# Flamingo block with WKV and a mixture of experts on one core: keys and y turned on VectorE by way of a scratch in memory

## The reference, cut to what matters

```python
def reference(x, ctx, g_xattn, g_ffn, time_decay, time_first, router, w_up_gate, w_down, shared_w_up_gate, shared_w_down):
    # x, ctx: (16, 256, 512)
    k = _layernorm(x)
    # WKV: per batch element and channel a scan over the 256 steps
    #   y_t = (a + exp(u + k_t) v_t) / (b + exp(u + k_t)),  a, b decayed sums of exp(k) v and exp(k)
    x = x + tanh(g_xattn) * _wkv(time_decay, time_first, k, ctx)
    z = _layernorm(x)
    # 4096 tokens: shared MLP 512 -> 2 * 1408 -> 512, and the best 2 of 8 experts, 512 -> 2 * 352 -> 512, by capacity
    x = x + tanh(g_ffn) * (shared(z) + routed(z))
    return x
```

## Time and profile before

| | |
|---|---|
| median of 3 runs | 1231.59 us (1231.01 to 1231.82) |
| profiled execution | 1232.66 us |
| its span in the trace | 1230.9 us |
| PE, DVE, POOL, ACT busy over the span | 1163.2, 682.7, 653.7, 509.6 us |
| granted clock of TensorE, mean | 0.99 |
| DMA | 232773 packets, 136.29 MB, 176477 packets under 512 B |

### The profile page before, as it was taken

One profiled execution on the slowest core, in us unless ns is written; L12 is line 12 of the kernel. 1 busy time (PEld: TensorE's weight loads), 2 busy tenths in 40 slices (PEclk: granted clock), 3 DMA queues, 4 the chain that ended last, 5 costly groups with the idle time before them and its releaser, 6 DMA issues. The chain is left out here.

```text
span 1230.9 us, 25978 instructions
## 1 busy us (share of the span) xinstructions
PE 1163.2 (94%) x8396; PEld 817.2 (66%) x8396; DVE 682.7 (55%) x1357; ACT 509.6 (41%) x915; POOL 653.7 (53%) x754
## 2 busy tenths in 40 slices
PE   1478999999999999999999989999999999999998
PEld 1366777777777777777776767566666666666653
DVE  6776787786786777776777866222222223222112
ACT  5665444443544443544534443333333333333220
POOL 7887457367457457456557542344444444444320
PEclk9998999999999999999999989999999999999999
DMA  8373232232222222222332323999899989997738
GB/s 234 92 206 72 53 70 53 53 69 52 54 66 52 60 61 55 68 49 60 87 69 48 59 65 62 204 178 180 173 169 172 176 171 165 178 169 130 127 50 319
DMA packets 232773, 136.29 MB, mean 111 GB/s; under 512 B 176477, under 2 KB 201077, under 8 KB 232544
## 3 DMA queue, kind: packets, MB, share of 16 engines
q1 hardware_dynamic: 213792, 97.55, 34.3%
q0 software_dynamic: 18048, 37.47, 17.6%
q10 hardware_dynamic: 832, 0.02, 0.0%
HBM read 69.83 MB, written 44.97 MB: 93 GB/s over the span
## 5 line engine op out<-in xcount | busy, mean ns | idle before, releaser
L1024 PE MATMUL PU<-xT,wreg 128*128 128x256 f16 x4224 | 504.5, 276 | 0.4 <-DVE srng L1311 0.4
L1024 PEld LDWEIGHTS PU<-xT,wreg 128*128 128x128 f16 x4224 | 415.1, 99 | 74.8 <-DVE srng L1311 0.7
L753 POOL DMA_INDIRECT moe_d<-wkv,acc x71 | 112.0, 1578 | 217.2 <-ACT wkv L928 214.2
L1131 PE MATMUL PU<-acc,wkv 128*128 x1284 | 214.5, 312 | 0.0
L1057 PE MATMUL PD<-wreg,hreg 128*128 128x512 f16 x858 | 206.4, 379 | 0.0
L634 POOL TENSOR_TENSOR hreg<-srng,hreg 128x256 f16<-128x256 f32 x165 | 134.6, 822 | 73.9 <-ACT hreg L850 72.9
L1131 PEld LDWEIGHTS PU<-acc,wkv 128*128 128x128 f16 x1284 | 125.1, 97 | 69.4
L1545 DVE TENSOR_TENSOR wkv<-PR,wkv 128x384 f16<-128x384 f32 x71 | 39.6, 557 | 208.1 <-ACT wkv L922 148.7
L1152 PE MATMUL PD<-acc,wkv 128*128 (+1 forms) x639 | 149.6, 379 | 1.5 <-DVE wkv L1545 1.5
L834 ACT ACTIVATE srng<-PU 128x256 f32<-128x256 f32 x176 | 66.7, 379 | 201.4 <-PE PU L1024 149.5
L1057 PEld LDWEIGHTS PD<-wreg,hreg 128*128 128x128 f16 x858 | 84.0, 98 | 73.5
(11 more groups left out here) (177 smaller groups left out, 1327.5 us busy)
## 6 DMA issues: line engine op xcount, KB each, us to landing
wreg<-in_L_ffn_w_up_gate SPq DMA_DIRECT2D x48, 176.0 KB
acc<-in_x SPq DMA_DIRECT2D x32, 256.0 KB, 3.0
xhl_d<-wkv SPq DMA_DIRECT2D x32, 256.0 KB, 2.3
wkv<-in_ctx SPq DMA_DIRECT2D x112, 64.0 KB, 2.4
moe_d<-acc SPq DMA_DIRECT2D x13, 512.0 KB
out<-moe_d SPq DMA_DIRECT2D x2, 3328.0 KB, 21.1
acc<-n_L_ffn_shared_w_up_gate SPq DMA_DIRECT2D x16, 256.0 KB, 5.7
wreg<-in_L_ffn_w_down SPq DMA_DIRECT2D x12, 256.0 KB
```

Of the source, the lines that this page charges most:

```text
L753: pool.indirect_dma_start(out=moe_d, out_offset=bass.IndirectOffsetOnAxis(ap=didx[:, t:t + 1], axis=0), in_=ostage[t % 3], in_offset=None, ...
L1024: mm = pe.matmul(PU[r][:, gu * UN:(gu + 1) * UN], sU[:, m, gu, a, kt, :], xT[:, u.par, b, kt, :], start=(kt == 0 and a + b == 0), stop=(kt ...
L1131: mm = pe.matmul(up_set[t % 2][gu][:, 0:I], xgT[:, t % 4, a, kt, :], weights(h, ((gu * 2 + b) * KT + kt) * I, P, I), start=(kt == 0 and a ...
```

## The change

Keys and y of units 2 to 15 are no longer turned by TensorE. `norm_k` and `divide` are followed by a store of the tile into a scratch in memory (`k_d`, `y_d`, one tile each), and by a load back into the same buffer (`kbuf`, `nd[:, 0]`) by four DMAs that swap the 32x32 blocks, as the values' load does. VectorE then turns the blocks into PT. Store and load are issued by SyncE, at slots of their own; the load waits for the store's semaphore. The table of stages is a new one for units 2 to 15; the first two units keep the old one (`FIRST_AT`). In the new table `stats_x`, `norm_k`, `turn_k`, `den`, `num` and `divide` come one to four slots earlier, `factors`, `turn_v` and `turn_k` of a unit stand closer together, and `norm_k` (k0) and `exp_k` (k1) of neighbouring units share S10.

```diff
-STAGE_AT = {
+FIRST_AT = {
     "stats_x": (-21, -16),
     "norm_k": (-19, -13),
     "turn_k": (-18, -12),
+    "exp_k": (-18, -12),
     "factors": (-16, -10),
     "turn_v": (-16, -10),
+    "load_v": (-16, -10),
     "den": (-14, -9),
     "num": (-13, -8),
     "divide": (-12, -7),
...
+STAGE_AT = {
+    "stats_x": (-24, -19),
+    "norm_k": (-23, -17),
+    "store_k": (-23, -17),
+    "load_k": (-22, -16),
+    "turn_k": (-19, -13),
+    "exp_k": (-18, -12),
+    "factors": (-18, -12),
+    "turn_v": (-18, -12),
+    "load_v": (-17, -11),
+    "den": (-16, -11),
+    "num": (-15, -10),
+    "divide": (-14, -9),
+    "store_y": (-14, -9),
+    "load_y": (-13, -8),
+    "turn_y": (-11, -5),
+    "add_y": (-10, -5),
+    "norm_x2": (-9, -4),
+    "split_x": (-8, -3),
+    "logits": (-6, -1),
+    "choose": (-6, 4),
+}
...
+            def load_blocks(buf, rows, landed):
+
+                for q in range(P // SQ):
+                    sp.dma_start(buf[q * SQ:(q + 1) * SQ, :].rearrange("p (k b j) -> p k b j", k=KT, j=SQ),
+                                 rows.rearrange("(b i) (k q j) -> q i k b j", i=SQ, k=KT, j=SQ)[q]).then_inc(landed, 16)
+
+            def store_k(c):
+                wait_alone(k_norm, c + 1)
+                sp.dma_start(k_d, kbuf).then_inc(k_out, 16)
+
+            def load_k(c):
+                wait_alone(k_out, 16 * (c + 1 - UT * PE_TURNED))
+                load_blocks(kbuf, k_d, k_in)
+
+            def store_y(c):
+                wait_alone(y_done, c + 1)
+                sp.dma_start(y_d, y_of_nd).then_inc(y_out, 16)
+
+            def load_y(c):
+                wait_alone(y_out, 16 * (c + 1 - UT * PE_TURNED))
+                load_blocks(y_of_nd, y_d, y_in)
...
+                    for v, k in tiles_at("load_k", u, s):
+                        load_k(v.tile(k))
+                    for v, k in tiles_at("load_y", u, s):
+                        load_y(v.tile(k))
+                    for v, k in tiles_at("load_v", u, s):
...
+                    for v, k in tiles_at("store_k", u, s):
+                        store_k(v.tile(k))
+                    for v, k in tiles_at("store_y", u, s):
+                        store_y(v.tile(k))
...
+            def turn_k(c):
+                wait_alone(k_in, 64 * (c + 1 - UT * PE_TURNED))
+                dve.wait_ge(x2_done, c - 1)
+                dve.transpose(PT[:, :], kbuf).then_inc(k_turned, 1)
+
+            def turn_y(u, k):
+                c = u.tile(k)
+                wait_alone(y_in, 64 * (c + 1 - UT * PE_TURNED))
...
+                dve.transpose(PT[:, :], y_of_nd).then_inc(y_turned, 1)
```

More of the change, by code:

```diff
@@ L72 @@
     "choose": (-6, 1),
+    "store_k": (), "load_k": (), "store_y": (), "load_y": (),
+}
[20 more added lines that the diff above has]
+    "choose": (-6, 4),
 }
@@ L131, with turned_by_pe @@
 LAST = [Route(GROUPS - 1, 14 * (GROUPS - 1), TILES - GT, UT, 0), Route(GROUPS, 14 * (GROUPS - 1) + 12, TILES - UT, UT, UT)]
+def turned_by_pe(u):
+    return u.fixed and u.v < PE_TURNED
 def tiles_at(stage, u, s):
-    return [(u.shift(-(o // JT)), k) for k, o in enumerate(STAGE_AT[stage])
-            if o % JT == s and u.shift(-(o // JT)).exists()]
+    found = []
+    for table, first in ((FIRST_AT, True), (STAGE_AT, False)):
+        for k, o in enumerate(table[stage]):
+            v = u.shift(-(o // JT))
+            if o % JT == s and v.exists() and turned_by_pe(v) == first:
+                found.append((v, k))
+    return found
 def key(u, s):
@@ L156, in build @@
         moe_d = nc.dram_tensor("moe_d", (NTOK + 4 * P, D), F32, kind="Internal").ap()
+        k_d = nc.dram_tensor("k_d", (P, D), F32, kind="Internal").ap()
+        y_d = nc.dram_tensor("y_d", (P, D), F32, kind="Internal").ap()
         slot_d = nc.dram_tensor("slot_d", (TRASH + TOPK * NTOK, 2), F32, kind="Internal").ap()
@@ L404, in load_ctx @@
                 else:
-                    for q in range(P // SQ):
-                        sp.dma_start(ctxb[r][q * SQ:(q + 1) * SQ, :].rearrange("p (k b j) -> p k b j", k=KT, j=SQ),
-                                     ctx_rows[bass.ds(c * P, P), :].rearrange("(b i) (k q j) -> q i k b j", i=SQ, k=KT, j=SQ)[q]
-                                     ).then_inc(v_in[r], 16)
+                    load_blocks(ctxb[r], ctx_rows[bass.ds(c * P, P), :], v_in[r])
             def load_u(m):
@@ L451, in unit @@
                         start_sums(u.shift(-2))
-                    for v, k in tiles_at("turn_v", u, s):
+                    for v, k in tiles_at("load_k", u, s):
[3 more added lines that the diff above has]
+                    for v, k in tiles_at("load_v", u, s):
                         if v.shift(1).exists():
@@ L860, in unit @@
                         norm_k(v.tile(k))
-                    for v, k in tiles_at("turn_k", u, s):
+                    for v, k in tiles_at("exp_k", u, s):
                         exp_k(v.tile(k))
@@ L971, in turn_y @@
                 pe.wait_ge(y_done, c + 1)
-                if u.fixed and u.v == UNITS - 1 and k == 1:
-                    pe.wait_ge(x2_done, c)
-                else:
-                    pe.wait_ge(ek_ready, c + 2)
-                turn(PT, nd[:, 0].rearrange("p k t -> p (k t)")).then_inc(y_turned, 1)
+                pe.wait_ge(ek_ready, c + 2)
+                turn(PT, y_of_nd).then_inc(y_turned, 1)
             def logits(u, k):
@@ L1064, in unit @@
                     for v, k in tiles_at("turn_k", u, s):
-                        turn_k(v, k)
+                        if turned_by_pe(v):
+                            turn_k(v, k)
                     def attend():
                         for v, k in tiles_at("turn_v", u, s):
-                            if v.fixed and v.v < PE_TURNED:
+                            if turned_by_pe(v):
                                 turn_v(v, k)
@@ L1084, in attend_late @@
                         for v, k in tiles_at("turn_y", u, s):
-                            turn_y(v, k)
+                            if turned_by_pe(v):
+                                turn_y(v, k)
                     if u.fixed and u.v < 0:
@@ L1264, in turn_v @@
                 dve.transpose(PR[:, :], ctxb[k]).then_inc(v_turned, 1)
+            def turn_k(c):
[5 more added lines that the diff above has]
+                wait_alone(y_in, 64 * (c + 1 - UT * PE_TURNED))
+                if u.fixed and u.v == UNITS - 1 and k == 1:
+                    dve.wait_ge(x2_done, c)
+                else:
+                    dve.wait_ge(ek_ready, c + 2)
+                dve.transpose(PT[:, :], y_of_nd).then_inc(y_turned, 1)
             def num(u, k):
@@ L1442, in unit @@
                             add_down(UT * (u.v - 2) + t, t, PD)
+                    for v, k in tiles_at("turn_y", u, s):
+                        if not turned_by_pe(v):
+                            turn_y(v, k)
                     for v, k in tiles_at("add_y", u, s):
@@ L1453, in unit @@
                         split_x(v, k)
+                    for v, k in tiles_at("turn_k", u, s):
+                        if not turned_by_pe(v):
+                            turn_k(v.tile(k))
                     for v, k in tiles_at("divide", u, s):
@@ L1464, in unit @@
                     for v, k in tiles_at("turn_v", u, s):
-                        if not (v.fixed and v.v < PE_TURNED):
+                        if not turned_by_pe(v):
                             turn_v(v, k)
```

2 lines of the change are left out of this document (added).

## The result

| | before | after |
|---|---|---|
| median of 6 runs each, side by side | 1231.70 us | 1313.60 us (1313.05 to 1314.39) |
| ratio, 95% interval | | 1.0667 [1.0655, 1.0678] |
| span of the profiled execution | 1230.9 us | 1311.7 us |
| granted clock of TensorE, mean | 0.99 | 0.958 |

The change costs 82 us, where 28 were forecast: right in its sign, three times too small in its size. The span grew by 80.8 us.

The account below looks back on a forecast made before the run. TensorE, busy all 45.3 us of a unit, was the bound; a new cycle of 47.3 us (units 2 to 12, +22), unit 14 +2, unit 1 +1, units -1 and 0 +3 gave +28: 1260 us, range 1214 to 1286.

Parts of the forecast that it names:

- The bound: Shared expert's stage: TensorE busy for all 45.30 us of a unit, so only its own work sets the pace.
- TensorE's saving: Four groups of transposes dropped per unit, 1.74 us; 56 groups in all, 24 us.
- VectorE's transposes: Four 128x512 transposes added per unit on VectorE, 0.73 us busy each; busy time up 41 us in all.
- The round trip: SyncE's store and four-piece load of finished y: 0.15 + 2.2 + 2.65 - 0.65 + 2.4, about 6.7 us.
- The rival of a dear round trip: Store and load dearer: +1 us for each of two waits a unit, +10 at the start; 1283 us, chance 0.13.
- The chain to the logits: From S6's up products through VectorE's S0, divide and SyncE's turn of x: logits of k0 start at 43.6 us.
- the four links above: Walked chain: VectorE's S0 at 22.4 us, divide's end 35.2, turn of x after pieces issued at 40.2, logits 43.6.
- the last link of the cycle: TensorE after k0's logits: 15 up products 1.64 us, six down products 1.3, so next S6 at 46.8 us.
- Units 2 to 12, eleven of them, at +2.0: Steady stage: each unit 47.3 us, 2.0 more than before, +22 us in all.
- the edges: Outside units 2 to 12: units -1 and 0 +3 us, unit 1 +1, unit 13 0, unit 14 +2.
- The Trainium skill's rule: Use TensorE for 128x128 transposes if PSUM is fine; the four groups would go back, a unit 45.3 us as before.

Follow-up runs that it names:

- the run with four edits: Changed kernel with turn of x ahead of load_y, sends moved to odd units, norm_k of k0 a slot later, inv_std ahead of add_den and add_num: 1266.1 us.
- The two artificial waits: Kernel before plus one TensorE wait in each of units 2 to 13, for one 64 KB store (1258.8 us) or two in series (1290.2 us).
- the mended order: Changed kernel with turn of x, load of y, norm_k, inv_std, routing and sends moved: 1241.6 us; with the last sends back in unit 12, 1235.7 us.
- the pairs above: Changed kernel at successive steps of mending its order, each with scratch and with TensorE turning keys and y: from 1313.6 against 1309.8 to 1235.7 against 1244.1 us.

## Why the prediction was wrong in its size

- **The bound**: right. TensorE was full, and what counted was the time at which its waits end.
- **TensorE's saving**, 1.74 us a unit: right; by the windows 452.4 - 17.2 is the work that is left. It shows as 43.5 us in the even units of the run with four edits.
- **VectorE's transposes** at 0.73: right (0.71 to 0.73). Its busy time rose by 31.8 us, where 41 were named, as each overlaps its neighbours (359.84 to 360.46 for one of 0.72, and the one before it ends at 359.92).
- **The round trip**: right. From the end of the divide (371.0) to the loads 2.2 us (2.35 summed), four pieces 2.63 (2.65), and 3.4 from the issue of the transpose to the logits (3.4); pieces land in 2.5. The rival of a dear round trip fell.
- **The chain to the logits**: right to within 0.5 us at each of the four links above in the even unit, with some luck in S6, as said there.
- **Where it failed, first: the last link of the cycle.** "15 up products 1.64, six down products 1.3" took the duration of a busy stage for products that start behind a wait. They took 4.61 and 5.71 us. In ten units these stretches are some 21 of the 24.4 us more of busy time, a term that the sum did not have. The two artificial waits show that it comes with the wait, in a kernel that is otherwise the one before. The trace of the kernel before already had it, right behind the two waits of the earlier trace rows:

```profile
96.06 6.31 PE L1024 MATMUL PU<-xT,wreg 128*128 128x256 f16 x33
102.21 0.60 PE L948 MATMUL PT<-ident,wkv 128*128 128x128 f32 x4
...
729.09 7.07 PE L1024 MATMUL PU<-xT,wreg 128*128 128x256 f16 x48
```

33 products in 6.15 us (96.06 to 102.21), 3.6 at the pace of the earlier trace rows, and 48 in 6.9 (to 735.99) instead of 5.24.
- **Second: a unit was taken for every unit.** "Units 2 to 12, eleven of them, at +2.0" is a walk through the even unit. In the odd one GpSimd's sends hold `hidden_lo`, ScalarE's silu waits 5.64 us for the buffer that it frees, and VectorE's S1 is late. Waits in ten units are 46.9 where the forecast had 37 (3.7 each), 9.9 more. Both together, 24.4 of busy and 9.9 of idle time, are the 34 us that ten units lie above the forecast's 20 (to rounding).
- **Third: the edges.** Up to the end of unit 1 +9.8, where units -1 to 1 had 4; unit 13 +6.9 where the prediction had 0; behind it +7.7 where unit 14 had 2. What makes up these three stays open. In the mended order, moving the last sends back changed unit 13 from 50.4 to 51.2 us and the time behind it from 549.6 to 543.7; in the changed kernel itself nothing was tried there, nor at the start.
- **The table was never priced alone.** The forecast walked new table and scratch as one chain. The run without scratch loses 79 us. The round trip of y lies on the walked path, but taking it away changes only 4 us, since TensorE's own transposes are back and `positions` waits (18.2 us for `ohx`, against 3.8).
- **The Trainium skill's rule** to leave a 128x128 transpose to TensorE (VectorE: DVE Perf Modes, Rules for kernel authors) was one of the ways in which the time could have come out. By the pairs above TensorE is 2 to 7 us ahead or level in all orders but the last, where it is 8 behind; neither decides the 82 us.
- **A slip in the rival of a dear round trip**: 1 us for each of two waits of a unit is 26 us in 13 units, not 13, and would make 1296. Nothing rests on it, as the round trip was not dearer.

## What to carry to other kernels

When a forecast adds a wait on the bounding engine, price the work behind it too: ask the trace what the same instructions take behind such a wait, and hold the lower clock as a term of its own. Walk the cycle once for each kind of unit: work that stands in every other unit, like sends or routing, belongs to a walk of its own. And before blaming a new operation, run the new order without it: here the order was the loss, and five small moves (load of y, `norm_k`, `inv_std`, routing, sends) gave back 78 of 82 us.

## What the runs showed of the hardware

- Granted clock over the 4 us behind a wait of TensorE, where it had been 1.00 in the 4 us ahead of the wait: 0.57 behind 3 of 12 waits of 1.9 us, 0.50 to 0.66 behind 9 of 12 of 3.5, and 0.50 over the 5.71 us behind one of 5.96. In the changed kernel all ten waits of units 3 to 12, 2.5 to 6.0 us long, have a fall behind them (0.50 to 0.66 up to the next S6). The fall can come within the wait: 0.52 from 326 to 330 us, ahead of the products at 330.36. 0.50 is the lower level, 1.2 GHz; the products were at full pace again 3.9 us behind the start of the first (309.49 to 313.43) and 5.9 behind that of the last (330.36 to 336.30).
- The price did not grow in proportion to the wait: 1.7 us in the even unit (4.61 for 2.93, behind 2.67 us of idling), as much behind the waits of 1.9 us with a fall and behind most of the 3.5 us ones (50.6 from logits to logits instead of 48.9), 2.5 behind another of these, 2.8 in the odd unit. The ten units have 1.5 to 2.8, and a wait of 2.96 us was followed by as dear a fall (682.30 to 687.98, 2.75) as one of 6.04.
- Sends by an indirect DMA keep GpSimd for 1.26 us each (308.40 to 309.66), so four in a row are 5 us in which nothing else of its program moves.
